# A small GpSimd write behind every indirect transfer of a two-layer mixture-of-experts program

## What is computed

```python
x = x + 0.5 * ffn(layernorm(x), ...)
x = x + attn(layernorm(x), Wq, bq, Wk, bk, Wv, bv, gamma, beta)   # windows of 128, top 32 scores
x = x + 0.5 * ffn(layernorm(x), ...)

def ffn(x, ...):                       # 8 experts, each token goes to the 2 with the largest router logits
    normed = (xt - mu) * rsqrt(var + eps) * ln_gamma + ln_beta
    logits = normed @ router_w.T
    top_v, top_i = top_k(softmax(logits), 2);  gates = softmax(top_v)
    for e in range(E):
        out = out + comb[:, e, None] * swiglu(normed, gate_up_w[e], down_w[e])   # 384 hidden columns
    out = out + swiglu(normed, shared_gate_up_w, shared_down_w)                  # 128 hidden columns
```

## Time and profile before

| | |
|---|---|
| median of three runs | 674.36 us (671.52 to 675.77) |
| the profiled execution | span 674.1 us, 15456 instructions |
| PE busy | 527.7 us (78%), 3928 instructions |
| DVE busy | 391.4 us (58%) |
| ACT busy | 337.5 us (50%) |
| POOL busy | 353.9 us (52%), 515 instructions |
| indirect stores, L1567 | 163, 159.6 us busy, 979 ns each |
| indirect scatters, L1539 | 128, 125.4 us busy, 979 ns each |

### The profile page before, as it was taken

How to read it: one execution, slowest core, us unless ns; L and a number is a source line. 1 busy time by engine, 2 the same in 40 slices (tenths; PEclk the granted TensorE clock), 3 DMA queues, 4 the chain that set the end, 5 groups by cost and what they waited for, 6 DMA issues and landing times.

```text
span 674.1 us, 15456 instructions
## 1 busy us (share of the span) xinstructions
PE 527.7 (78%) x3928; PEld 472.9 (70%) x3928; DVE 391.4 (58%) x1785; ACT 337.5 (50%) x816; POOL 353.9 (52%) x515
## 2 busy tenths in 40 slices
PE   3756888787789998978896259696789887899882
PEld 2535777677778897867784258676578777899872
DVE  5576655531164886974894768678768351222454
ACT  3534444363344876744865158474554463454431
POOL 1445556565664346555274704546567666555332
PEclk9878999999998999999997669988699898999987
DMA  6915545465575454663220453411354665676894
GB/s 199 301 33 189 187 161 191 160 232 190 197 266 186 173 185 154 224 209 133 99 91 33 121 172 113 152 72 67 133 178 160 214 187 194 229 247 226 284 303 148
DMA packets 88019, 117.88 MB, mean 175 GB/s; under 512 B 11848, under 2 KB 60880, under 8 KB 87936
## 3 DMA queue, kind: packets, MB, share of 16 engines
q1 hardware_dynamic: 76208, 96.75, 42.6%
q0 software_dynamic: 9312, 19.16, 8.2%
q10 hardware_dynamic: 2416, 0.99, 0.6%
HBM read 26.57 MB, written 26.19 MB: 78 GB/s over the span
## 4 chain that ended last, share of the span: by engine, by line
PE 43%; issue 13%; DVE 12%; ACT 10%; another core or an unknown queue 9%; DMA 4%; POOL 4%; SPq 2%; ACTq 1%; DVEq 1%; POOLq 0%
PE ps_y L731 10%; PE ps_g L717 8%; PE ps_h L722 5%; PE ps_u L722 4%; DVE xres L1307 2%; PE w L629 2%; PE w L659 2%; PE ps_x L711 2%; PE w L660 2%; POOL rows L1539 2%; DMA xin<-rows 2%; PE w L615 1%; ACT zz L844 1%; PE w L675 1%
## 5 line engine op out<-in xcount | busy, mean ns | idle before, releaser
L1567 POOL DMA_INDIRECT results<-raw_gu,idx x163 | 159.6, 979 | 188.2 <-ACT raw_gu L940 127.2
L731 PE MATMUL ps_y<-dn_t,raw_gu 128*128 x978 | 145.9, 287 | 36.4 <-ACT raw_gu L940 27.0
L731 PEld LDWEIGHTS ps_y<-dn_t,raw_gu 128*128 128x128 f32 x978 | 126.2, 197 | 48.1 <-issue 47.0
L1539 POOL DMA_INDIRECT rows<-zz,s_idx x128 | 125.4, 979 | 42.6 <-issue 34.1
L717 PE MATMUL ps_g<-x_t,raw_dn 128*128 128x128 f32 x978 | 141.9, 283 | 1.5 <-issue 1.5
L717 PEld LDWEIGHTS ps_g<-x_t,raw_dn 128*128 128x128 f32 x978 | 127.5, 199 | 3.6 <-issue 3.4
L940 ACT COPY raw_gu<-ps_y 128x128 f32<-128x128 f32 x163 | 42.9, 263 | 148.1 <-PE ps_y L731 70.2
L1380 DVE TENSOR_TENSOR raw_gu<-sil,ps_u 128x384 f32<-128x384 f32 x82 | 45.2, 551 | 91.3 <-PE ps_u L722 26.6
L934 ACT ACTIVATE sil<-ps_g 128x384 f32<-128x384 f32 x163 | 80.0, 491 | 35.7 <-PE ps_g L717 17.8
L930 ACT ACTIVATE x_t<-ps_x,bf_c,gf_c 128x128 f32<-128x128 f32 x163 | 75.3, 462 | 42.6 <-PE ps_x L711 32.3
L1380 DVE TENSOR_TENSOR raw_gu<-sil,ps_h 128x384 f32<-128x384 f32 x81 | 44.7, 552 | 84.5 <-PE ps_h L722 27.5
(11 more groups left out here) (166 smaller groups left out, 747.4 us busy)
## 6 DMA issues: line engine op xcount, KB each, us to landing
raw_dn<-gu_t SPq DMA_DIRECT2D x163, 384.0 KB
xin<-rows SPq DMA_DIRECT2D x163, 64.5 KB
yg<-results SPq DMA_DIRECT2D x15, 512.0 KB
results<-raw_gu,idx POOLq DMA_INDIRECT x163
rows<-pads SPq DMA_DIRECT2D x40, 64.5 KB
rows<-pads SPq DMA_DIRECT2D x5, 451.5 KB
rows<-zz,s_idx POOLq DMA_INDIRECT x128
out<-xres SPq DMA_DIRECT2D x7, 256.0 KB
```

Source lines behind the costliest of these rows:

```text
L731: t = pe.matmul(ps_y[:, 0, :], h_t[:, k4, c * P:(c + 1) * P], dn[:, bass.ds(off + c * D, D)], start=(c == 0), stop=(c == FC - 1))
L1539: pool.indirect_dma_start(xs, bass.IndirectOffsetOnAxis(s_idx[n][:, c, k:k + 1], 0), zz[n][:, k, c, :], None).then_inc(scat[n], 16)
L1567: pool.indirect_dma_start(yt, bass.IndirectOffsetOnAxis(idx[:, ky:ky + 1], 0), yb[:, ky, :], None).then_inc(yst[ky], 16)
```

## The change

A tile `still` of two times 200 integers in each partition and a semaphore `rested` are added. Behind every indirect transfer GpSimd writes 200 integers per partition into one half of the tile (`iota`), alternating between the halves. Before the n-th such write it waits until write n-2 is done. Nothing reads the tile. It adds 291 instructions to POOL, 128 behind the scatters and 163 behind the stores, and changes nothing else.

```diff
+        still = sb("still", [P, 2, 200], I32)
...
+            rests = itertools.count()
+
+            def apart_in_time():
+
+                n = next(rests)
+                if n >= 2:
+                    pool.wait_ge(rested, n - 1)
+                pool.iota(still[:, n % 2, :], pattern=[[1, 200]], base=0, channel_multiplier=0).then_inc(rested, 1)
+
             def number(R, n, tile):
...
                         pool.indirect_dma_start(xs, bass.IndirectOffsetOnAxis(s_idx[n][:, c, k:k + 1], 0),
                                                 zz[n][:, k, c, :], None).then_inc(scat[n], 16)
+                        apart_in_time()
                         turn()
...
                     pool.indirect_dma_start(yt, bass.IndirectOffsetOnAxis(idx[:, ky:ky + 1], 0),
                                             yb[:, ky, :], None).then_inc(yst[ky], 16)
+                    apart_in_time()
```

More of the change, by code:

```diff
@@ L340, in macaron @@
         lr_done, rr_done, rn_done, rg_done, x2_done = (sem(n) for n in ("lr_done", "rr_done", "rn_done", "rg_done", "x2_done"))
-        out_st, spare = sem("out_st"), sem("spare")
+        out_st, spare, rested = sem("out_st"), sem("spare"), sem("rested")
         passed = {e: sem(f"passed_{n}") for e, n in (
```

## The result

The changed kernel takes **645.3 us** (median of four runs, 641.4 to 648.0) against 673.8 (four runs, 671.5 to 675.8): a ratio of 0.959, 95% interval 0.954 to 0.964. I had forecast 666 us with a range of 648 to 692. The sign was right, but the gain is 28.5 us and not 8, and the time lies outside the range. The profiled execution after is the fastest of its four (641.4 us, span 639.5), so the two profiles differ by 34.6 us, more than the medians do.

The account below looks back on a forecast made before the run. TensorE's own work was 43% of the span; its late news behind close GpSimd transfers, 9% of the chain, was the target. 674.1 - 13.5 regained + 5.5 path cost = 666 us, range 648 to 692.

Parts of the forecast that it names:

- The cap: Down projection waiting for ScalarE's copy, 24 waits: 27.0 us, the most the change could give back; half, 13.5, expected.
- A threshold between 1.5 and 1.7 us: Distance between GpSimd's indirect transfers, or somewhat above, beyond which TensorE's news was expected to come on time.
- the 1.69: Transfer distance in us at which ScalarE's copy came without a wait, 0.19 us after a down-projection group's end; one case.
- the third step's scatter: Layer 1, on the chain from first to last transfer: 8.85 us before, forecast 10.8, 2.4 us of added cost.
- The write: 200 integers on GpSimd behind each of 291 transfers: 0.42 us forecast, range 0.29 to 0.69, from start-up writes.
- The distances: Between starts of GpSimd's transfers: 1.54 us forecast in a run instead of 1.27, 1.74 over a copy instead of 1.32.
- The cost on the path: Longer transfer runs on the chain: 2.4 and 1.8 us for two scatters, 1.3 for smaller delays, together 5.5 us.
- The added wait: GpSimd's write n waits for write n-2, already finished before transfer n-1 starts; costed at nothing.
- Rival 1: Late TensorE news unrelated to transfer distance, or 1.54 us not enough: only cost left, 680 us; chance 0.27.
- the 2.16 us of the earlier trace: Lateness of TensorE's news to ScalarE: down-projection group due to end at 158.49, copy started only at 160.65.
- Rival 2: GpSimd becomes the bound if a write takes 0.69 us, deciding from about 0.5: 700 us; chance 0.17.
- Rival 3: All of TensorE's late news disappears at a write that still fits GpSimd's idle time: 653 us; chance 0.13.

## Why the prediction was wrong in its size

**The cap was the step that failed.** Of the 27.0 us I wrote "This is the most that I let the change give back", and half of it, 13.5 us, was the gain in the sum. That row itself behaved nearly as forecast: 27.0 became 10.4 (15.1 and 17.8 in the two later profiles), where I had said 10 to 15. But it is one engine's wait for one other. The same late updates held ScalarE (101.0 us of "remote" waits before, 33.0 after), and through it routing and GpSimd's stores (127.2 us of waiting for ScalarE before, 50.3 after). A better first size stood in the earlier trace rows: 9% of the chain, 62 us. I had argued it away with "TensorE goes on with queued work in the meantime". The runs give more still: the unchanged kernel takes 598 us in the condition without late updates and 674 to 684 in the one with them, 76 us or more. (It was not profiled in the first; that nothing was late there is taken from the eight variants that ran beside it.) The change gets back 28.5 us net, or about 48 gross if the 3% that its writes cost without late news (1.017 and 1.015 for its two halves, added) holds here too; that sum is worked out, not measured. With 300 integers 36 us came back net.

**A threshold between 1.5 and 1.7 us was the wrong picture.** I read one limit out of the earlier trace rows and let each pair pass or fail. The lateness builds up along a run of close transfers. Worked out from the traces, the mean of the largest lateness of matmul groups that end in the 1.2 us after the start of a transfer, for the transfer that starts a run and for the second, third and fourth of the run (a run being transfers within 1.8 us of the one before):

```
                          first  second  third  fourth
before                    0.04   1.27    2.23   2.98
16 integers, chip 3       0.04   0.99    1.56   2.02
100 integers, chip 3      0.08   1.27    1.61   1.81
200 integers, the result  0.02   0.31    0.65   1.00
200 integers, chip 3      0.03   0.53    1.31   1.46
200 integers, chip 11     0.02   0.54    1.21   1.44
300 integers, chip 3      0.03   0.21    0.27   0.21
```

The group of the earlier trace rows ended at 509.85, before the second transfer of its run started at 509.91, so it was punctual not for the 1.69 alone. Wider distances lower the lateness in a run, at the fourth transfer with every size, at the second steadily only from 200 integers on. That the gain is gradual over the sizes fits this. Nor did only distances over 1.6 give something back: with the write behind the scatters alone, which leaves the distance behind a store as it was and makes that in the third step's scatter 1.50, the ratio was 0.978.

**The write.** I took 0.42 us; it lasted 0.312, near the lower end of 0.29. GpSimd's busy time grew by 87 us (353.9 to 441.3), not 122. The slope that I took from the starts of the writes of 8 and of 31 numbers was too steep: 16 to 400 integers give 0.158 to 0.478, 0.0008 us a number. The durations in the same rows, 0.15 for 15 numbers and 0.17 for 31 (152 and 166 ns in the trace), would have given an estimate of 0.31. The line of the Trainium skill that I had set beside it (GPSIMD Engine Reference, "Engine selection", near 0.25 us by my estimate) speaks of elementwise work with one input, which a counted pattern does not have; it erred on the other side, by 0.06 where I erred by 0.11. The distances came out at 1.50 and 1.61 instead of 1.54 and 1.74.

**The cost on the path.** The third step's scatter takes 10.54 us from first to last transfer, where I had said 10.8. The added wait costs nothing, as forecast. That 5.5 us in all were too few is likely: where nothing is late the two halves of the change cost 7 to 10 us each and the fill behind all transfers 15.0. What the cost is with late news was not taken apart. (The forecast's own range is also off by a little: three quarters and a quarter of the 27.0 give 659 to 673, not 658 to 674.)

**The rivals.** Rival 1 (only the cost is left, 680 us) is wrong for the result and right for the other condition. There no recorded update of TensorE is late in any of eight profiles, at mean distances of 1.28 to 1.68 us in the third step's scatter. The rule of the Trainium skill that I had named with it (SBUF — State Buffer, "Who interferes with whom") is about the ports of on-chip memory: TensorE and ScalarE wait on nobody there. The traces agree, since in the kernel with the write behind the stores one matmul of the down projection takes 284 ns and one SiLU 491 in either condition. Of late updates the section says nothing, so I was wrong to set it against the 2.16 us of the earlier trace rows. Rival 2 did not happen at 200 integers; with 400, at 0.48 us a write, GpSimd shares the chain with TensorE. Rival 3 (653 us, all late news gone) came nearest in time for a wrong reason: 3% of the chain and 193 late updates, 250 us of lateness in all, are still there. Only 300 integers come near to it.

## What to carry to other kernels

When the chain names a releaser that cannot exist, do not cap the gain at the wait of the one engine where it was first seen. Its share of the chain is a better first size, though no bound: it was 62 us here, the two conditions differ by 76, and with 100 integers the share stood at 10% while the time had fallen by 2.7%. Ask of every row of waits who else waits for the same news.

Measure a change on more than one chip and at more than one time, always beside the unchanged kernel. This change gains about 4% where the unchanged kernel takes 674 to 684 us. Where it takes 598 the whole change was not run; its parts lose 1.2 to 1.7% each and the fill behind all transfers 2.6%. Neither kernel is the better one in general: of what was tried, 300 integers are best in the first condition, no write at all in the second.

## What the runs showed of the hardware

- TensorE's updates reach the other engines within 0.02 us (eight profiles) or, under one condition, late by 2.98 us on the mean around the fourth transfer of a run, depending on how closely GpSimd's indirect transfers follow each other and for how long. Four of the six batches showed this, on chips 3, 5, 11 and 15, as did the result's own runs; two did not, on chips 1 and 15. Chip 15 showed both. What sets the condition is open: no kernel of this study turned it on or off, and the profile names no cause. The mean granted clock does not tell them apart (the kernel with the write behind the stores has 0.926 late and 0.936 punctual, the result's two profiles have 0.926 and 0.936 as well, both late).
- One mark in the traces does tell the conditions apart, in all twenty profiles. With late news the trace holds only 68 to 75% of the semaphore updates that the instructions of TensorE, ScalarE, VectorE and GpSimd make, without it 99.5% or more; of DMA landings it holds about 5300 to 5900 against 10700 to 10900. So the loss goes with the condition and not with the distances: 300 integers heal nearly all of the lateness and leave the trace at 75%. Every timed run on record comes with a span and a clock from the profiler, so no run tells whether the condition also exists when no profile is taken, or whether the recording of updates is itself what makes them late. That rival is untested.
- That the lateness is a backlog, of descriptors, of their completions or of the profiler's records, would fit how it builds up along a run. It was only argued.
- An indirect transfer of 128 rows keeps GpSimd for 0.98 to 1.01 us on the mean; behind it an `iota` of 16, 100, 200, 300, 400 integers takes 0.158, 0.227, 0.311, 0.394, 0.478 us, and a fill of 200 floats 0.28.
- In a run of transfers the distance grows by less than the write: from 1.27 to 1.51, 0.24, for a write of 0.31, since part of the pause that stood between two transfers before takes the write in. For the fill it is 0.17 for 0.28.
